# Attention steps of a fused Perceiver block: the output's transposes put ahead of the scores on TensorE, and VectorE's order rearranged around them

## The reference, cut to what matters

```python
x = x + cosine_similarity(layernorm(x) @ Wv.T + bv, ctx @ Wt.T + bt)   # 64 x 64 x 256
# attention over 64 sequences of 64 rows, 16 heads of 16
q, k, v = proj(layernorm(x))
attn = softmax(q @ k.T / sqrt(16))
o = attn @ v
align = sum(o * v, -1) / (sum(v * v, -1) + 1e-8)
o = o - align * v
x = x + o @ wo.T + bo
# top-1 mixture of 14 experts, 256 -> 512 -> 256
e = argmax(layernorm(x) @ router_w); p = softmax(...)[e]
x = x + p * (gelu(layernorm(x) @ w1[e] + b1[e]) @ w2[e] + b2[e])
```

## Time and profile before

| | us |
|---|---|
| median of 3 runs | 522.25 (520.49 to 522.72) |
| the profiled execution | 520.23 |
| its span (first to last instruction) | 518.3 |

### The profile page before, as it was taken

One profiled execution on the slowest core, in us unless ns is written; L12 is line 12 of the kernel. 1 busy time (PEld: TensorE's weight loads), 2 busy tenths in 40 slices (PEclk: granted clock), 3 DMA queues, 4 the chain that ended last, 5 costly groups with the idle time before them and its releaser, 6 DMA issues.

```text
span 518.3 us, 14429 instructions
## 1 busy us (share of the span) xinstructions
PE 501.0 (97%) x4324; PEld 397.7 (77%) x4325; DVE 346.2 (67%) x1054; ACT 347.1 (67%) x837; POOL 240.9 (46%) x405
## 2 busy tenths in 40 slices
PE   8999999999999999999999999899999999999993
PEld 6555555566788888888878888778989999999992
DVE  4578666647899989898998889997562333323231
ACT  3777777668988888889888888886444333343430
POOL 2366555335434545564555546551763232333332
PEclk9999999999999999999999999999999999999997
DMA  8954446101002223322332232247667666666520
GB/s 301 370 205 147 160 153 208 58 1 32 12 23 57 74 89 113 111 81 89 113 104 74 71 82 74 62 131 230 203 199 230 219 207 208 220 187 212 191 82 9
DMA packets 35617, 69.88 MB, mean 135 GB/s; under 512 B 5664, under 2 KB 23714, under 8 KB 35568
## 3 DMA queue, kind: packets, MB, share of 16 engines
q1 hardware_dynamic: 31680, 60.19, 37.2%
q0 software_dynamic: 3456, 8.85, 4.6%
q10 hardware_dynamic: 432, 0.26, 0.2%
HBM read 54.21 MB, written 11.60 MB: 127 GB/s over the span
## 4 chain that ended last, share of the span: by engine, by line
PE 85%; DVE 7%; issue 4%; POOL 1%; ACT 1%; DMA 1%; DVEq 0%; POOLq 0%; ACTq 0%
PE psum L1392 13%; PE psum L1405 12%; PE psum L1327 8%; PE psum L1278 6%; PE psum L1165 6%; PE psum L1286 5%; PE psum L1299 5%; PE psum L1340 4%; PE psum L1246 4%; PE psum L1208 3%; PE psum L1215 3%; PE psum L1177 3%; PE psum L1191 3%; PE psum L1219 3%; PE psum L1180 3%
## 5 line engine op out<-in xcount | busy, mean ns | idle before, releaser
L1392 PEld LDWEIGHTS psum<-arena,ring 128*128 128x128 f32 x640 | 77.3, 192 | 3.5 <-issue 1.7
L1392 PE MATMUL psum<-arena,ring 128*128 128x128 f32 x640 | 78.2, 275 | 0.9 <-ACT arena L1109 0.6
L1405 PE MATMUL psum<-w_s,arena 128*128 x320 | 76.0, 381 | 0.0
L929 DVE TENSOR_TENSOR arena<-psum,tok 128x256 f32<-128x256 f32 x40 | 17.0, 424 | 84.8 <-PE psum L1405 83.1
L1103 ACT ACTIVATE arena<-psum 128x256 f32<-128x256 f32 x40 | 15.4, 384 | 86.6 <-PE psum L1165 56.3
L1405 PEld LDWEIGHTS psum<-w_s,arena 128*128 128x128 f32 x320 | 57.8, 190 | 6.5
L490 POOL TENSOR_TENSOR ov<-o_n,v_s 128x256 f32<-128x256 f32 x32 | 23.5, 734 | 80.1 <-DVE o_n L694 80.1
L1073 ACT ACTIVATE arena<-kT,head_mask 128x256 f32<-128x256 f32 x128 | 57.4, 501 | 0.0
L545 POOL DMA_INDIRECT out<-arena,token_of x40 | 39.9, 998 | 19.9 <-POOL token_of L537 14.1
L1109 ACT ACTIVATE arena<-psum,b_s 128x128 f32<-128x128 f32 x160 | 45.4, 374 | 3.7 <-PE psum L1392 2.2
L797 DVE TENSOR_REDUCE smax<-psum 128x16 f32<-128x1024 f32 x32 | 39.0, 1218 | 2.8 <-PE psum L1299 1.6
(11 more groups left out here) (193 smaller groups left out, 1122.5 us busy)
## 6 DMA issues: line engine op xcount, KB each, us to landing
ring<-w SPq DMA_DIRECT2D x40, 512.0 KB, 3.6
w_s<-ctxT SPq DMA_DIRECT2D x15, 768.0 KB, 4.6
w_s<-w SPq DMA_DIRECT2D x16, 448.0 KB, 3.5
slot_rec<-routed SPq DMA_DIRECT2D x40, 132.0 KB, 3.3
tok<-x SPq DMA_DIRECT2D x16, 256.0 KB, 4.7
v_swap<-v_s SPq DMA_DIRECT2D x64, 64.0 KB
routed<-pad_rec SPq DMA_DIRECT2D x1, 1980.0 KB, 10.8
tok<-b SPq DMA_DIRECT2D x14, 128.0 KB, 3.3
```

What stands on the lines that cost most here:

```text
L1392: mm = pe.matmul(hid_bank(p)[:, f * P:(f + 1) * P], w1_s[:, r, c * F + f * P:c * F + (f + 1) * P], xgT[:, p, c * P:(c + 1) * P], start=c = ...
L1405: mm = pe.matmul(bank(2 + q, D), hidT[:, q, f * P:(f + 1) * P], w2_s[:, bass.ds(e * (FC * D) + f * D, D)], start=f == 0, stop=f == FC - 1)
```

## The change

* PE: `all_scores()` moves from before `turn_output` to behind it, in every step. The script of the last tiles (after step 32) stays as it is.
* DVE: `o_n` moves from behind `rec` and `logit` to right behind `rsum`. `xn` moves from behind the statistics to behind `coef`, and the wait for the statistics to before `dot`. `o_f` moves from behind `v_s` to before `bn_aggr` and `v_s`. The addition of epsilon to `vvsum` (L793) goes: `vv` gets a 17th column for each head, which holds epsilon, and the sum runs over 17.
* The settling of a group is spread over two steps: `lcs`, `ranked`, `esum` and `earlier` stay in step k % 4 == 0; `rank`, `posf`, `pos`, `lsum` and its inverse move to the step after it (k % 4 == 1, called "late" here), `lsum` and `posf` to before `o_f`.
* POOL: the wait `settled` of the loop moves from the head of the step to behind `along` and the gather's work, right ahead of the bias addition L510. Written-out steps have it in `send`, behind L510, before and after. One `memset` of the epsilon column is added in the cosine stage.
* ACT and SP: `v_swap` and its 64 transfers go; ACT reads `v_s` in the other half of the partitions instead.

```diff
-                if live(i):
-                    need(sp, s["val_ok"], i + 1)
-                    need(sp, s["vd_ok"], i - 1)
-                    for b in range(2):
-                        sp.dma_start(v_swap[(1 - b) * S:(2 - b) * S, p, :], v_s[b * S:(b + 1) * S, k, :])\
-                            .then_inc(swap_in[p], 16)
...
-                if not isinstance(x, int):
-                    settled(x, (k - 9) % RING)
                 if live(y):
                     need(pool, s["on_ok"], y + 1)
                     pool.tensor_tensor(ov[:, :], o_n[:, :], v_s[:, (k - 3) % 4, :], ALU.mult).then_inc(s["ov_ok"], 1)
...
+                if not isinstance(x, int):
+                    settled(x, (k - 9) % RING)
                 if live(i):
 
                     need(pool, s["xn_ok"], i + 1)
...
-                    need(pool, s["vvsum_raw"], i)
-                    pool.tensor_tensor(vv[:, :], v_s[:, k % 4, :], v_s[:, k % 4, :], ALU.mult).then_inc(s["vv_ok"], 1)
+                    need(pool, s["vvsum_ok"], i)
+                    v_i = v_s[:, k % 4, :].rearrange("p (h d) -> p h d", h=NH)
+                    pool.tensor_tensor(vv[:, :, 0:HD], v_i, v_i, ALU.mult).then_inc(s["vv_ok"], 1)
...
-                settle, shares = settle and "routes" in parts, settle and "probs" in parts
+                late = live(i - 6) and k % GROUP == 1 and "late" in parts
+                sums = settle and ("sums" in parts or "routes" in parts)
+                settle, shares = late or settle and "routes" in parts, late or settle and "probs" in parts
                 aside = dict(aside)
-                done = slice(k % RING, k % RING + GROUP)
+                first = (k - k % GROUP) % RING
+                done = slice(first, first + GROUP)
                 of_group = i - 3
-                of_last = i - 4
+                of_last = i - 4 - k % GROUP
...
                 if live(y):
                     need(dve, s["o_psum"], y + 1)
                     dve.reciprocal(rsum[:, :], o_ps[:, :, HD]).then_inc(s["rsum_ok"], 1)
+                if live(y):
+                    need(dve, s["rsum_ok"], y + 1)
+                    dve.tensor_tensor(o_n[:, :].rearrange("p (h d) -> p h d", h=NH), o_ps[:, :, 0:HD],
+                                      rsum[:, :].unsqueeze(2).broadcast_to([P, NH, HD]), ALU.mult)\
+                        .then_inc(s["on_ok"], 1)
...
-                if live(w):
-
-                    need(dve, s["stats3_raw"], w + 1)
...
-                if live(t) and not (isinstance(t, int) and t in (1, 2)):
-                    normalise(t, (k + 1) % 2)
...
+                if sums:
                     dve.tensor_reduce(esum[:, :], onehot[:, :, :].rearrange("p t e -> p e t"), AX.X, ALU.add)\
                         .then_inc(s["esum_ok"], GROUP)
                 if "weighing" in aside:
                     aside["weighing"]()
+                if live(w):
+                    need(dve, s["stats3_raw"], w + 1)
                 if live(y):
                     need(dve, s["ov_ok"], y + 1)
                     dve.tensor_reduce(dot[:, :], ov[:, :].rearrange("p (h d) -> p h d", h=NH), AX.X, ALU.add)\
...
                     dve.tensor_tensor(coef[:, :], dot[:, :], rvv[:, (k - 3) % 4, :], ALU.mult).then_inc(s["coef_ok"], 1)
+                if live(t) and not (isinstance(t, int) and t in (1, 2)):
+                    normalise(t, (k + 1) % 2)
...
-                    dve.tensor_reduce(vvsum[:, :], vv[:, :].rearrange("p (h d) -> p h d", h=NH), AX.X, ALU.add)\
-                        .then_inc(s["vvsum_raw"], 1)
+                    dve.tensor_reduce(vvsum[:, :], vv[:, :, :], AX.X, ALU.add).then_inc(s["vvsum_ok"], 1)
...
+                if shares:
+                    need(dve, s["expl_ok"], of_last)
+                    dve.tensor_reduce(lsum[:, :], expl[:, :, :], AX.X, ALU.add).then_inc(s["lsum_ok"], GROUP)
+                if live(y):
+                    need(dve, s["along_ok"], y + 1)
+                    need(dve, s["oT_psum"], y - 1)
+                    dve.tensor_tensor(o_f[:, (k - 3) % 2, :], o_n[:, :], along[:, :], ALU.subtract).then_inc(s["of_ok"], 1)
                 if live(w):
                     dve.bn_aggr(rec[:, r, R_MEAN:R_MEAN + 2], stats3[:, :]).then_inc(s["stats3_ok"], 1)
+                if settle:
+                    need(dve, s["posf_ok"], of_last)
+                    dve.tensor_scalar(pos[:, done, 0], posf[:, :], float(E * REGION), None, ALU.add)\
+                        .then_inc(s["pos_ok"], GROUP)
+                if shares:
+                    need(dve, s["lsum_ok"], of_last)
+                    dve.reciprocal(rec[:, done, R_PROB], lsum[:, :]).then_inc(s["prob_ok"], GROUP)
                 if live(i):
                     need(dve, s["val_psum"], i + 1)
                     need(dve, s["along_ok"], i - 3)
                     dve.tensor_tensor(v_s[:, k % 4, :], bank(6, D), bv_s[:, :], ALU.add).then_inc(s["val_ok"], 1)
...
-                if live(y):
-                    need(dve, s["along_ok"], y + 1)
-                    need(dve, s["oT_psum"], y - 1)
-                    dve.tensor_tensor(o_f[:, (k - 3) % 2, :], o_n[:, :], along[:, :], ALU.subtract).then_inc(s["of_ok"], 1)
-                if shares:
-                    need(dve, s["expl_ok"], of_last)
-                    dve.tensor_reduce(lsum[:, :], expl[:, :, :], AX.X, ALU.add).then_inc(s["lsum_ok"], GROUP)
-                if settle:
-                    need(dve, s["posf_ok"], of_last)
-                    dve.tensor_scalar(pos[:, done, 0], posf[:, :], float(E * REGION), None, ALU.add)\
-                        .then_inc(s["pos_ok"], GROUP)
...
-                if live(u):
-                    need(dve, s["vvsum_raw"], u + 1)
-                    dve.tensor_scalar(vvsum[:, :], vvsum[:, :], ATT_EPS, None, ALU.add).then_inc(s["rvv_raw"], 1)
...
-                if shares:
-                    need(dve, s["lsum_ok"], of_last)
-                    dve.reciprocal(rec[:, done, R_PROB], lsum[:, :]).then_inc(s["prob_ok"], GROUP)
                 if live(u):
-                    need(dve, s["rvv_raw"], u + 1)
+                    need(dve, s["vvsum_ok"], u + 1)
                     dve.reciprocal(rvv[:, (k - 1) % 4, :], vvsum[:, :]).then_inc(s["rvv_ok"], 1)
...
-                need(act, swap_in[q], arrivals(u, q, 2, 32))
+                need(act, s["val_ok"], u + 1)
                 need(act, s["o_psum"], u - 1)
...
-                act.activation(vd[S:P, q, 0, :, HD + 1:VW - 1], heads(v_swap[S:P, q, :], 1), ACT.Copy)
-                act.activation(vd[0:S, q, 1, :, 0:HD], heads(v_swap[0:S, q, :], 0), ACT.Copy)
+                act.activation(vd[S:P, q, 0, :, HD + 1:VW - 1], heads(v_s[0:S, r, :], 1), ACT.Copy)
+                act.activation(vd[0:S, q, 1, :, 0:HD], heads(v_s[S:P, r, :], 0), ACT.Copy)
...
-                all_scores()
                 if live(y):
                     need(pe, s["xT_ok"], i + 1, NT)
                     turn_output(y, (k - 3) % 2)
+                all_scores()
                 if live(w) and k % GROUP == GROUP - 1:
                     need(pe, s["on_ok"], v)
                     rank_group(w)
```

More of the change, by code:

```diff
@@ L205, in build @@
         v_s = sb("v_s", [P, 4, D])
-        v_swap = sb("v_swap", [P, 2, D])
-        vv = sb("vv", [P, D])
+        vv = sb("vv", [P, NH, HD + 1])
         vvsum = sb("vvsum", [P, NH])
@@ L277, in build @@
         ctx_in = [sem(f"ctx_in{n}") for n in range(4)]
-        swap_in = [sem(f"swap_in{n}") for n in range(2)]
         rec_out = [sem(f"rec_out{n}") for n in range(RING)]
@@ L288, in build @@
             stats_raw stats_ok vareps_ok rstd_ok xn_ok xT_psum xT_ok qk_psum k_ok q_ok
-            val_psum val_ok vv_ok vvsum_raw rvv_raw rvv_ok vd_ok kd_ok s_psum smax_ok centred exp_ok pT_psum pT_ok
+            val_psum val_ok vv_ok vvsum_ok rvv_ok vd_ok kd_ok s_psum smax_ok centred exp_ok pT_psum pT_ok
             o_psum rsum_ok on_ok ov_ok dot_ok coef_ok along_ok of_ok oT_psum oT_ok wo_psum x3_ok
@@ L417, in later_consts @@
                     pool.iota(token_ids[:, :], [[P, NT]], base=0, channel_multiplier=1).then_inc(s["consts_made"], 1)
+                elif i == 3:
+                    pool.memset(vv[:, :, HD], ATT_EPS).then_inc(s["mask_made"], 1)
                 elif i == 2:
@@ L656, in context_step, with attention_step @@
                     ones_of_values()
-            def attention_step(i, k, parts=("tile", "ranked", "lcs", "routes", "probs"), aside=()):
+            def attention_step(i, k, parts=("tile", "ranked", "lcs", "sums", "late"), aside=()):
                 t, u, y, w, z = i + 1, i - 1, i - 3, i - 4, i - 5
@@ L691, in attention_step @@
                         .then_inc(s["logit_ok"], 1)
-                if live(y):
-                    need(dve, s["rsum_ok"], y + 1)
-                    dve.tensor_tensor(o_n[:, :].rearrange("p (h d) -> p h d", h=NH), o_ps[:, :, 0:HD],
-                                      rsum[:, :].unsqueeze(2).broadcast_to([P, NH, HD]), ALU.mult)\
```

(3 more changed lines are left out.)

## The result

The median went from 522.15 us (519.88 to 523.45, 6 runs) to 545.68 us (544.2 to 546.42, 6 runs): 1.0462 of the time before, 95% interval 1.0442 to 1.0481. The forecast was 540, 526 to 546: the direction and the mechanism came out, and the size lies at the upper edge (545.68 is 0.3 inside it; the ratio 1.0462 on the 522.25 us from which the range was worked out is 546.4, 0.4 outside). The span of the profiled execution is 543.9 us against 518.3 of before, 25.6 more (the medians differ by 23.5), where the sum had 18.6.

A forecast was written before the change was run, and what follows sets the result against it. PE bounds the attention stage; with the new order its scores wait for `o_f`, closing a dependency loop. Terms of +3.4, +13.0 and +2.2 us make +18.6: 538.8 from the profile, 540.9 from the median, said 540, range 526 to 546.

The forecast's parts named there:

- The circle: Attention step: `smax`, `o_n`, `ov`, `coef`, `along`, `o_f`, transposes, scores, next `smax`; a floor of 7.45 us against PE's 7.30.
- bare circle: Attention step with `o_f` not held by POOL: plain steps 7.45 us; as rival 526 to 533 us, chance 0.23.
- The hold: POOL's bias addition L510 starts before `o_f` and holds it: 0.93 us, ending at 6.34, plain step 7.98.
- sum over four steps: Attention loop: plain 7.98, late 7.95, gather 8.0, settle 8.15, together 32.1 us against 29.73, 0.59 more a step.
- planned steps: Two steps with slot planning: `o_f` already bounds and is held; +1.1 us each after 0.42 credit for `o_n`, +2.2 together.
- first five of the 29: Steps before the first settling: 7.98 us for 7.30 each, +3.4 us together.
- Settle: Steps k % 4 == 0: `lcs` ends with `ov`, two short operations add 0.17; 8.15 us, addition between 0 and 0.4.
- rival "worse": `xn` held in every step, short two-input operations held, or exponential late: another 0.3 us a step, over 546; chance 0.06.
- Gather: Steps k % 4 == 3: `o_f` not held, but `xn` and others ahead; 7.9 or 8.25 by `xn`'s start, taken as 8.0.
- `o_n` ahead: DVE: `o_n` right behind `rsum`, ahead of `rec` and `logit`, gives the chain 0.4 us; 0.42 credited in steps with planning.
- plain and late steps: Attention loop: plain 7.98 us with `o_f` held; k % 4 == 1 taken as 7.95, `o_f` not held in the loop.
- What was called nothing: `v_swap` transfers, epsilon addition and 17th column, later L811, moved `settled` wait, memset and PE's clock: no cost or gain.

The follow-up runs named there:

- e4: Changed kernel with POOL's bias addition moved to the end of its step and `xn` moved behind `o_f`; 528.33 us, 1.0139 of before.
- e7: Changed kernel with only `xn` moved behind `o_f`; 545.66 us, 1.0263 of the kernel before on that chip.
- e8: Changed kernel with only `earlier` moved behind `o_f`; 553.09 us, 1.0373 of the kernel before on that chip.
- e9: Changed kernel with only `o_n` put back behind `rec` and `logit`; 554.71 us, 1.0418 of the kernel before on that chip.
- e6: Kernel before with only the `v_swap` copy and the addition of epsilon removed; 527.79 us, 0.9924 of before on that chip.
- e11: Kernel before with only the `v_swap` copy and the addition of epsilon removed, repeated on another chip; 527.75 us, 0.9912 of before.
- e5: Changed kernel with PE's old order, POOL's bias addition last in its step and `xn` behind `o_f`; 528.85 us, 0.9942 of before.
- e2: Kernel before with only PE's order changed, `turn_output` ahead of `all_scores`; 552.33 us, 1.0599 of before.

## What the prediction had right, and the step of it that failed

The circle, its links and its floor were right: PE waits for `o_f` in all 29 steps, it runs the same 4324 matmuls, the plain steps of e4 take the 7.45 us of the bare circle, and undoing the swap (e1) takes the whole cost back. The hold was right too: `o_f` takes 0.90 to 0.93 us wherever it starts 0.1 us or less behind L505 (written-out plain steps, and e7). What failed is the sum over four steps, 32.1 us or 0.59 more a step: it measured 32.9 to 33.2, because the settle and gather terms were too small, and the planned steps' term was too small as well. The page SBUF — State Buffer of the Trainium skill, section Who interferes with whom, says that the two engines shut each other out from a shared port; the trace agrees for `o_f`, `earlier` and `xn`. Its clause that the first one keeps the port can't be read off start times that lie close together: `xn` starts 0.02 us ahead of `along` in the plain row above and is the one held (0.79 us). Where it starts 0.16 ahead, in the written-out plain steps, it takes 0.41, and `along` takes 0.72 us instead of 0.62.

By steps: the first five of the 29 cost 3.8 us (3.4 forecast), the 22 of the groups 17.2 (13.0), the two with planning 3.4 (2.2), and 1.1 came ahead of the first `smax` and 0.2 behind the last (none forecast). The terms that were mis-sized:

* **Settle, 8.61 to 8.69 and not 8.15.** The text set 0.17 for "two short ones" behind `lcs` and did not look at `earlier`, behind `coef`. Its hold of 0.53 us makes 0.41 of the 0.5 (e8). The rival "worse" named it ("short two-input operations held in each") and gave it 0.06. The row for it was there: the earlier trace rows has `posf`, 4 elements, at 0.39 us.
* **Gather, 8.5 in two and 8.3 in two, not 8.0.** The text had 7.9 if `xn` starts before `along` and 8.25 if after, and took 8.0. `xn` is held in every gather step of the loop (start 231.40, `along` 231.41, 0.78 us). The two of 8.3 are near the branch of 8.25; `coef` comes 4.70 after `smax` in them, instead of 4.50. `dot` waits behind `lc` and starts 4.24 after `smax` instead of 4.06. In the two of 8.5 `coef` is later still, at 231.16, 4.92 after its `smax` (226.24): `cand` stands between `dot` (230.48) and it, 0.68 from start to start instead of 0.44. Moving `xn` away gives 7.67 to 7.92 (e7).
* **The planned steps.** The text put no cost on the clock. The 1.32 us wait of before left it at 1.00, but here, behind waits of 0.76 and 1.74 us, it fell, in a step of 10.84 where before's 8.66 + 1.1 = 9.76 was forecast. e8, with the same `o_f` and no drop, has 10.31 there, so 0.53 of the 1.08 us is the clock. Of the rest, 0.32 is the start of `o_f`: 7.50 us after `smax`, where 7.60 of before less the credit of 0.42 for `o_n` is 7.18. The last 0.23 lies between the scores and `smax`, 1.39 us in e8 for the usual 1.16, and is not explained.
* **`o_n` ahead** is worth 0.24 us in a plain step and 0.23 in the planned one (10.54 in e9 against 10.31 in e8), not 0.42. The circle had 2.67 for its start (measured 254.05 - 251.37 = 2.68): the credit in the planned steps was too large, the circle was not.

The plain and late steps, 8.00 and 8.01, were forecast at 7.98 and 7.95, the plain one of the loop by luck, on another way: `xn`'s hold and `vvsum` in place of `o_f`'s whole hold. So `o_f` is at 0.9 us in the written-out plain steps only and at 0.60 in one of the loop's four, where the text had 0.9 in two of four. What was called nothing was nearly nothing, but for the clock: with PE's old order, the removed copy, the epsilon and the rest come to 0.8 us together (e1), though the copy and the epsilon alone made the stage 1.6 to 2.1 us longer (e6, e11). The 1.1 us ahead of the first `smax` (123.2 against 122.1) are not explained, but they do not go with the new order: e7, e8 and e9, which have it too, have their first at 122.3 to 122.5, and e5, with the old one, at 123.2.

## What to carry to other kernels

Before a wait of one engine is moved ahead of some of its work, look whether what it waits for depends, through the other engines, on that same work of the step before. If it does, the wait is no gap that can be filled but part of a circle, whose links can be summed from one timeline, and whose sum is a floor under the step. Here PE had 7.30 us of its own work, the circle 7.45, and the order with slack (scores first) hid nearly every delay of DVE. When a circle sets the time, every instruction between its links counts, the tiny ones too, and two delays that overlap come free only together.

The shortest attention steps of the study are those of e1, the changed kernel with the old order of PE: 227.9 us, 0.9982 of the time before. The lower ratios, down to 0.9912 (e11), were measured on slower chips and do not come from the attention steps.

## What the hardware showed that was not expected

* An addition of 14 bf16 elements on DVE took 0.69 us beside an addition of 256 columns on POOL, and 0.16 away from it. It ended 0.03 us after POOL's instruction; `o_f`, with 256 columns, ended 0.27 us after it (257.71 against 257.44). So the hold lasted to the end of POOL's instruction for the short one as for the long one.
* `xn`, with one tensor in SBUF and two values per partition, took 0.78 to 0.79 us beside `along` when its start was 0.01 to 0.03 us ahead of it, 0.41 when it was 0.16 ahead, and 0.40 to 0.41 behind `o_f` (e7).
* PE at granted clock 1.00, busy 3.50 of 6.00 us, dropped to 0.54 in the following 3.7 us, with waits of 0.76 and 1.74 us before. In e2 it fell in the same step, to 0.50 behind a wait of 2.34 us. But e9, with a wait of 2.12 us there, e8 with 0.49 and 1.75, and e7 with 1.56 kept 1.00 throughout the stage, so the length of the last wait alone does not tell whether the clock falls.
* The kernel before took 520.9 us on one chip and 532 to 535 on three others. The attention steps that an edit left alone took the same time on all of them; what was longer lay behind the last `smax`, 170.6 to 177.9 us instead of 167.9.
